# State-space mixer with attention and experts: the products of the heads taken eight slots at a time, with twelve decay buffers

## The reference

```python
zxbcdt = x @ W_in.T                         # z, xBC and dt
xBC = silu(causal_conv(xBC, conv_w))        # 4 taps
dt = softplus(dt_raw + dt_bias)
cum = cumsum(dt * A)                        # per head, in a chunk
Lmat = exp(where(tril, cum_i - cum_j, -inf))
M = (C @ B.T) * Lmat * dt                   # 128 x 128 per head
Yd = einsum('bcijh,bcjhp->bcihp', M, xs)    # the "products of the heads"
# plus the state carried from chunk 0 to chunk 1, D * xs, the gate silu(z),
# an RMS norm and @ W_out.T
```

## Time and profile before

| | |
|---|---|
| profiled execution, whole time | 1391.03 us |
| its span, first to last instruction | 1389.1 us |
| median of three runs | 1391.88 us |
| mean granted clock of TensorE | 0.966 |
| TensorE busy | 1285.0 us, 93% |
| VectorE busy | 819.5 us, 59% |
| ScalarE busy | 698.1 us, 50% |
| GpSimd busy | 583.1 us, 42% |

### The profile page before, as it was taken

One profiled execution on the slowest core, in us unless ns is written; L12 is line 12 of the kernel. 1 busy time (PEld: TensorE's weight loads), 2 busy tenths in 40 slices (PEclk: granted clock), 3 DMA queues, 4 the chain that ended last, 5 costly groups with the idle time before them and its releaser, 6 DMA issues.

```text
span 1389.1 us, 23017 instructions
## 1 busy us (share of the span) xinstructions
PE 1285.0 (93%) x7655; PEld 729.7 (53%) x7655; DVE 819.5 (59%) x1838; ACT 698.1 (50%) x1334; POOL 583.1 (42%) x871
## 2 busy tenths in 40 slices
PE   6799999999999999888888878989999999999996
PEld 4567667676767666543434333334444444444443
DVE  5898988888888877578888997561111111111111
ACT  2768686868686866735878766621111111111110
POOL 1475657666656556752333452431222222222221
PEclk9999999999999999987999998969999999999999
DMA  9100000000000001002111100023244344334222
GB/s 343 34 9 21 9 21 9 20 9 21 9 21 9 21 9 28 1 5 102 36 36 36 36 30 35 9 74 120 58 138 139 66 129 138 90 94 137 46 46 31
DMA packets 49554, 77.33 MB, mean 56 GB/s; under 512 B 19168, under 2 KB 32224, under 8 KB 48416
## 3 DMA queue, kind: packets, MB, share of 16 engines
q1 hardware_dynamic: 39504, 52.43, 11.0%
q0 software_dynamic: 8736, 20.61, 7.9%
q10 hardware_dynamic: 1200, 2.82, 0.5%
HBM read 152.97 MB, written 20.25 MB: 125 GB/s over the span
## 4 chain that ended last, share of the span: by engine, by line
PE 67%; DVE 16%; issue 6%; ACT 5%; POOL 3%; DMA 1%; SPq 1%; POOLq 0%; DVEq 0%; ACTq 0%
PE work_ps L573 12%; PE gate_ps L1575 10%; PE up_ps L1575 10%; PE down_ps L1559 9%; PE work_ps L639 7%; PE work_ps L578 4%; PE work_ps L1091 3%; DVE conv L760 3%; DVE maxes L1265 2%; PE mturn_ps L578 2%; PE work_ps L659 2%; DVE decay L756 2%; PE work_ps L1082 2%; PE work_ps L647 1%; ACT prob L1163 1%
## 5 line engine op out<-in xcount | busy, mean ns | idle before, releaser
L573 PE MATMUL work_ps<-xnT,w_in 128*128 128x256 f32 (+1 forms) x1216 | 290.0, 387 | 4.8 <-DVE xdt L890 2.8
L573 PEld LDWEIGHTS work_ps<-xnT,w_in 128*128 128x128 f32 (+1 forms) x1216 | 228.0, 193 | 58.7 <-issue 21.5
L756 POOL TENSOR_TENSOR decay<-decay,cbm 128x512 f32<-128x512 f32 x128 | 185.8, 1453 | 138.5 <-ACT decay L751 135.0
L1663 POOL DMA_INDIRECT out_dram<-y_out,ids x39 | 61.9, 1587 | 334.8 <-DVE row_w L1627 230.1
L1265 DVE TENSOR_REDUCE maxes<-work_ps 128x2 f32<-128x512 f32 x256 | 166.0, 681 | 31.3 <-PE work_ps L1067 30.2
L1163 ACT ACTIVATE prob<-work_ps 128x512 f32<-128x512 f32 x256 | 142.4, 609 | 73.6 <-PE work_ps L1082 72.8
L1642 DVE TENSOR_TENSOR act<-gelu,up_ps 128x512 f32<-128x512 f32 x39 | 26.8, 687 | 251.9 <-PE up_ps L1575 251.9
L751 ACT ACTIVATE decay<-decay 128x512 f32<-128x512 f32 x256 | 161.6, 639 | 12.9 <-DVE xnT L1214 5.4
L747 ACT ACTIVATE decay<-work_ps 128x512 f32<-128x512 f32 x256 | 138.7, 600 | 37.4 <-PE work_ps L647 36.9
L1575 PE MATMUL gate_ps<-w_e,xgT 128*128 x312 | 140.5, 593 | 1.4 <-ACT xgT L1592 1.0
L1559 PE MATMUL down_ps<-w_e,actT 128*128 x312 | 140.5, 593 | 0.8 <-ACT actT L1605 0.8
(11 more groups left out here) (267 smaller groups left out, 1918.5 us busy)
## 6 DMA issues: line engine op xcount, KB each, us to landing
w_e<-c_experts_dram SPq DMA_DIRECT2D x39, 3072.0 KB
normed_tokens<-r_xn SPq DMA_DIRECT2D x17, 256.0 KB, 2.1
out_dram<-x_sb SPq DMA_DIRECT2D x17, 256.0 KB, 2.5
eexp<-ecum_scratch SPq DMA_DIRECT2D x64, 64.0 KB
x_sb<-x_dram SPq DMA_DIRECT2D x1, 3072.0 KB, 17.5
w_in<-c_w_inT_dram ACTq DMA_DIRECT2D x1, 2560.0 KB, 11.7
w_in<-c_w_inT_dram SPq DMA_DIRECT2D x1, 2048.0 KB, 9.8
w_out<-c_w_outT_dram SPq DMA_DIRECT2D x1, 2048.0 KB, 23.0
```

Source lines behind the costliest of these rows:

```text
L573: m = e.matmul(ps[0:width, at:at + L], w_in[:, k, col:col + width], xnT[b % 2][:, k, :], start=(k == 0), stop=(k == KD - 1))
L756: return e.tensor_tensor(four(decay[s % NDECAY]), four(decay[s % NDECAY]), cb, ALU.mult)
```

## The change

Before, at every fourth slot `i` the list held the heads of the four tiles `i-8` to `i-5` (two pieces), and then four decay products. Now the heads stand only at slots with `i % 8 == 4`, and there they are those of the eight tiles `i-12` to `i-5` (four pieces): a whole unit. There are twelve decay buffers where there were ten.

```diff
-NDECAY = 10
+NDECAY = 12
...
     for i in range(NS_STEPS + 2 * GROUP):
         if i % GROUP == 0:
-            for s in range(i - 2 * GROUP + 1, i - GROUP, 2):
-                if s >= 0:
-                    put(i, ("heads", s))
+            if i % NHALF == GROUP:
+                for s in range(i - 3 * GROUP + 1, i - GROUP, 2):
+                    if s >= 0:
+                        put(i, ("heads", s))
             for s in range(i, min(i + GROUP, NS_STEPS)):
                 put(i, ("decay", s))
```

## The result

The changed kernel takes 1402.07 us (median of nine runs, 1395.62 to 1408.14), beside 1389.64 us for the kernel before (nine runs, 1383.06 to 1392.44). The ratio is 1.0111 with a 95% interval of 1.0089 to 1.0133: slower by 1.1%, where 0.3% was forecast. The predicted 1395.0 us is 7 us short, and the range ended at 1402. The profiled execution took 1401.40 us, its span is 1399.3 us against 1389.1 before.

What follows compares the result with a forecast made beforehand. A batch was taken as bound by VectorE from slot 14 to 25 (14.51 us) and by TensorE otherwise (55.15). Six batches at 0.70 us (+4.2) and -0.3 in the last gave +3.9 to 4.0 on 1391.03: 1395.0 us, range 1384 to 1402.

Steps and rivals of the forecast that it cites:

- The switches: Heads' rounds on TensorE: a double round takes 1.89 us, a unit 2.09 instead of 2.22 us, a gain of 0.13.
- TensorE's part of a batch: From slot 25 to the next slot 14, bound by TensorE: 0.62 + 0.08 = 0.70 us more a batch.
- the wait for `dt_exp`: In slot 9 it moves from the state product to the z product behind it, losing 0.08 us a batch.
- VectorE's part: From slot 14 to slot 25, bound by VectorE's unbroken row: 14.51 us of a batch, nothing gained there.
- The wait in slot 24: TensorE waits there before `out` for `yz`, 2.0 us in one piece, where it waited 0.6 + 0.2.
- rival B: After slot 24's 2.0 us wait TensorE's granted clock falls, losing 3.4 us each time; chances 0.07 and 0.06 by count.
- One or two falls: The granted clock falls behind slot 24's wait in one or two batches: 1398 to 1402 us, chance 0.07.
- all six: The granted clock falls behind slot 24's wait in each of six batches: +20.4 us, 1415 us, chance 0.06.
- The last batch: Behind TensorE's release at 506.80, two single rounds go and two become double: -0.3 us, then VectorE's attention pieces set the pace.
- The first batch: It ends in VectorE's part, so its rounds are absorbed: 0.
- the first TensorE part behind it: First of six stretches from slot 25 to the next slot 14, each priced at +0.70 us.

Runs made afterwards that it cites:

- main_fill: main_double with the fourth decay product of slot 24 done eight times over in the first six batches: 1389.69 us, ratio 0.9995 to the kernel before.
- main_double: The kernel before with the change's double rounds for units 0 to 25 only, single ones for the last six: 1398.03 us, ratio 1.0088.
- main_double_again: main_double once more, on another chip, beside main_fill: 1396.37 us, ratio 1.0054 to the kernel before.
- double_u2: The kernel before with twelve decay buffers and a double round only for the third unit of each batch (slot 28): 1392.02 us, ratio 1.0062.
- tail_double: The kernel before with double rounds for units 26 to 31 only: 1391.14 us, ratio 1.0033.
- tail_last: The kernel before with double rounds for units 29 to 31 only: 1390.31 us, ratio 1.0002.
- tail_first: The kernel before with double rounds for units 26 to 28 only: 1385.36 us, ratio 0.997.

## Why the prediction was wrong

**The switches, right.** The double round takes 1.89 us as worked out.

**TensorE's part of a batch, right.** In slot 9 the wait for `dt_exp` stands before L574, as expected, 0.35 us long. The timeline of TensorE in the changed kernel:

```profile
341.98 1.02 PE L623 MATMUL work_ps<-xw,b_tok 128*128 128x512 f32 x2
343.36 1.99 PE L574 MATMUL work_ps<-xnT,w_in 128*128 128x256 f32 x8 [0.35 <-ACT dtT L685]
```

A batch of the change without a fall (the first `out` of slot 24, 376.94 to 447.27) lasts 70.33 us against 69.66 before: +0.67 for the predicted +0.70. By the marks, five batches of main_fill take 3.0 us more, 0.6 each. With the first of the six parts (below) all six cost 4.8 us instead of 4.2.

**VectorE's part, right.** Its row from slot 14 to `yz` has not changed: from start to start it takes 12.87 us in one batch of the changed kernel and 12.93 in the same batch of before (286.67 to 299.60). In the changed kernel, from 291.51 to 304.38:

```profile
291.51 1.26 DVE L761 SCALAR_TENSOR_TENSOR conv<-work_ps,conv_w,conv 128x255 f32<-128x255 f32 x3
...
304.38 0.69 DVE L911 TENSOR_TENSOR yz<-yz,zs 128x512 f32<-128x512 f32 x1
```

The wait in slot 24 stands before `out` and is 1.71, 2.66, 2.07, 2.07, 1.76 and 2.06 us long in the first six batches, on the average as forecast (2.0). It was right that the time taken from TensorE there came to nothing, and wrong to stop there: the wait was costed as idle time alone.

**The clock, the step that failed.** The sum of the forecast has no term for it: it stood apart as rival B, mis-sized in its chance, its count and its price. "One or two falls" had 0.07 and "all six" 0.06. The profiles of the change and of the kernels that have its slot 24 (main_double, main_double_again, double_u2) show two, three, four and three falls. A fall costs 1.7 us, not 3.4: the batch that starts with one lasts 72.03 us (233.18 to 305.21) instead of main_fill's 70.34, and 6.5 us divided by four falls is 1.6. The 3.4 us came from a stretch with two waits in a row. The reason given against B, a wait of 1.79 us that left the clock at 1.00, was one observation below the forecast length of 2.0, and I read it as covering it. The runs put 0.6% (8 us) on it: main_double_again against main_fill.
The Trainium skill, "TensorE: Matmul & The Clock Gate", section "Why this matters for your kernels", warns of idle gaps between bursts of products, though of longer ones than the waits of slot 24. Here the trace agrees on the clock, with a granted 0.89 in windows with a fall and 1.00 with the gap filled, and shows it behind shorter gaps. In the timed pair the clock is about half of the 1.1%; in the profiled execution of the change it is 3.4 of 13.6 us by tile 15.

**The last batch, wrong in sign: the second step that failed.** The step "-0.3, and then the attention's pieces on VectorE set the pace" priced two rounds as if TensorE were busy there. In units 29 to 31 it waits around nearly every round, so a single round beside a wait is free, and a double one elsewhere is not. Measured: +3 to +6 us from tile 11 to 15, part of it the clock's, 0.33% in tail_double's total, and 5.0 us between tail_last and tail_first.

**The first batch, right, and the first TensorE part behind it, too low.** The marks to tile 1 look scattered (main_double and main_double_again, the same kernel, differ by 1.5 us) because the mixer starts at a different time in each profile. Counted from the decay products of slot 4, at 50.72 before, they aren't. The timeline of TensorE in the changed kernel:

```profile
51.04 0.60 PE L648 MATMUL work_ps<-RT,LT 60*128 60x512 bf16 x4
```

From there the first `out` of slot 24 starts 40.14 us later before (90.86) and 40.24 in the change (91.28): the first batch loses 0.1 us, where 0 was predicted. The mark of tile 1 comes 91.16 us later before and 92.96 in the change. In the other kernels whose first batch has single rounds it is 91.00 to 91.19, in those with double ones throughout 92.95 to 92.97 and, with the casts moved, 92.42. So the first of the six TensorE parts cost 1.7 us, where 0.70 was predicted; what makes the other microsecond wasn't traced. To tile 11 it is 443.51 before, 448.32 in main_fill and 451.69 in the change: 4.8 us for the rounds, 3.4 for two falls.

**Sum.** Predicted +3.9. Measured in the profiled executions until tile 15: 0.3 ahead of slot 4, 4.8 for the rounds of the first six batches, 3.4 for two falls, 5.1 in the last two, 13.6 in all. So the rounds were priced nearly right, and what failed is the clock, left out of the sum, and the last batch, put at -0.3. The two parts timed alone, 1.0054 to 1.0088 and 1.0033, make 0.9 to 1.2%, which is the 1.1% of the whole. One thing doesn't close: main_fill keeps the 4.8 us of the rounds at tile 11, and yet its total shows at most 0.18% (2.5 us) by its interval. Against tail_first on the same chip it takes 4.3 us more, which would fit; why before is slow on that chip stays open.

## What to carry to other kernels

Before a round is taken out of a slot, ask whether the engine waits there: work beside a wait is free, and merged with other work elsewhere it is paid in full, so that fewer mode switches cost more time. When an edit lengthens a wait of TensorE, price the clock behind it as a term of the sum, with a chance for each place where the wait occurs. To test it, fill the wait with repeated products and look at the granted clock: it is a change of a few lines that leaves the order as it is.

## What the runs showed of the hardware

- Single waits of about 2 us in a stretch that is otherwise 98% busy lowered the granted clock in most batches but not in all: behind 12 of 20 slots 24 in four profiles (the change, main_double, main_double_again, double_u2). The length doesn't decide it. Waits of 1.76 us (377.28 in main_double_again) and 2.07 us (233.18 and 305.21 in the change) were followed by a fall; waits of 1.76 (376.94), 2.06 (447.27) and 2.66 us (162.84), all in the change, were not.
- A fall costs 1.6 to 1.7 us, about what one group of four `out` products loses at 1.2 GHz (3.42 us instead of 1.79).
- Useless products in a wait can pay: seven extra ones on 60 rows in each of six waits took 0.59% off the time of this kernel.
